# A macaron layer with a state-space scan on one core: tanh for silu, and products with tokens on partitions

## The chip, the core and the metric

The kernel runs on one core of a Trainium2 chip. Its engines are TensorE (PE), VectorE (DVE), ScalarE (ACT), GpSimd (POOL) and SyncE (SP), which issues transfers. The metric is the device time of one launch in microseconds (us), smaller is better. The time before is 2232.82 us, the median of 3 runs (2228.62 to 2250.01).

## The reference, cut to what matters

32 sequences of 256 tokens with 128 channels go through three layers, each behind a layer norm and added to its input: half an FFN, a Mamba block, half an FFN (the same weights both times). All of it is float32.

```
ffn(x):    router = x @ Wg ; top_logits, idx = top_k(router, 2)          # of 8 experts
           w = scatter(softmax(top_logits))                              # (tokens, 8)
           h = silu(x W1[e]) * (x W2[e])          # 8 experts of 176 hidden columns
           y = sum_e w[:, e] * (h W3[e]) + (silu(x Ws1) * (x Ws2)) Ws3   # shared: 352 columns
mamba(x):  x_in, z = split(x W_in + b_in)                                # 256 channels each
           xc = silu(causal_conv4(x_in) + conv_b)
           B, C = split(xc W_xp + b_xp) ; delta = softplus(xc W_dt + b_dt)
           h_t = exp(delta_t A) h_{t-1} + delta_t xc_t B_t               # 16 states
           y = (sum_states(h_t C_t) + D_skip xc) * silu(z)
           return layernorm(x + y W_out + b_out, alpha, beta)
x = x + 0.5 ffn(norm(x)) ; x = x + mamba(norm(x)) ; x = x + 0.5 ffn(norm(x))
```

## The kernel before, in words

**Tiling.** Two sequences, 512 tokens, are one group; there are 16 groups, and nearly all products have their 512 tokens as columns. Pass k works on five groups at once: FFN 1 of group k+2 (the diff says it `enters`), the projections of the Mamba block of k+1 (`lead`), the scan of k (`scans`), the output projection of k-1 (`tail`) and FFN 2 of k-2 (`last`). Passes -2 to 1 and 14 to 17 are written out and only partly filled; passes 2 to 13 are full and run in a hardware loop of two passes an iteration.

**A pass has 32 slots.** Each engine runs its own program of the same slots, and semaphores tie them together. In each pair of slots one of the 16 scan states is worked on: at the start of the even slot PE lays the row of B out over the partitions (`row_b`, L1012, into `ps_db`); DVE multiplies it with `du` at the end of the slot before (`input_term`, L834, which waits for the row), runs the scan (L868) in the even slot, and GpSimd multiplies with the row of C (`prod`, L569). ScalarE makes the decays, two Exp a state (L657).

**FFN units.** The hidden columns of an FFN are 14 chunks: 3 of shared columns, then 11 of experts. One chunk is a unit and starts in each of slots 0 to 13 (FFN 2) or 14 to 27 (FFN 1). In its slot PE makes `ps_h1` (L1030) and `ps_h2` (L1048), each a 512-column product into one of two banks, and ScalarE makes `silu` from `ps_h1` (L680). One slot later DVE makes `gated`: `ps_h2` times the routing weights `wrow` for an expert chunk, times silu for a shared one (L860). Two slots later GpSimd multiplies an expert chunk with silu (the join, L521). Four slots later PE adds the down product (L1043) to `ps_y`, channels on partitions. `ps_h1` is free for the next but one unit when silu has read it, `ps_h2` when DVE has.

**Other steps** are put in slots by a table written by hand, `PLAN` (and `SP_PLAN` for transfers). In a slot each engine first does the scan's and the unit's work, then the steps of the table in their order. Nearly all of PE's other products (`xT`, `logits`, `wT`, `in0` to `in3`, `dt`, `xproj`, `cT`, `bT`, `outproj`, `outT`, `yT`) go to one PSUM bank, `ps_m`: PE claims it for a step only when the step before in the table has been read out (`claim` waits for `misc_taken`), and the reader waits for `misc_full`. The steps that the change touches:
- `y0`/`y1` (ACT, L730): copies `ps_y` to `yT`; `yT0`/`yT1` (PE): four transposes; `addy` (DVE, L926): adds half of it to `xres`.
- `in0`, `in1` (x_in with the convolution as four shifted products, L1003, and an edge product) and `in2`, `in3` (z): ScalarE makes silu of them straight from `ps_m`.
- `outproj` (PE, L1110, two products of 512 columns with channels on partitions; ACT copies to `oT` and adds `b_out`), `outT` (four transposes), `resid` (DVE, L961, adds it to `rtok`), `stats3` (DVE).
- `x1n` (ACT): makes the normalised input of the Mamba block once more, into `rtok`.
- `dt0`, `dt1`: softplus on ScalarE: Abs (L752) and Identity (L750) of each half, Exp (L756), and in the next slot Ln (L668).
- `route` and `weights`: the two largest logits, and the softmax of them. GpSimd makes the power of e (L542), DVE the sum (L912), the quotient and two products.

Exp, Ln and silu need tables in ScalarE; where the next function is in another set than the one loaded, an ACT_TABLE_LOAD stands ahead of it in the program.

## Time and profile before

| | |
|---|---|
| median of 3 runs (range) | 2232.82 us (2228.62 to 2250.01) |
| profiled execution: time, span | 2241.29 us, 2239.5 us |
| mean granted TensorE clock | 0.887 |
| busy share PE / DVE / ACT / POOL | 80% / 73% / 69% / 64% |
| chain that ended last | PE 43%, ACT 21%, DVE 17%, issue 12% |
| instructions | 22836 |

Read the shares with care: an engine with 70% may be full in one stretch of a pass and idle in the next, so the page's first part names the candidates, and the windows over one pass show which engine is full where. In the timeline, the time in square brackets is how long the engine stood idle before the row, and behind it what it waited for.

### The profile page before, as it was taken

The page shows a single profiled execution, that of the slowest core. Times are in us where ns is not written, and L with a number is a line of the kernel's source. Part 1 is how long each engine was busy: PE and PEld are TensorE (multiplying, and loading weights), DVE is VectorE, ACT ScalarE, POOL GpSimd, SP SyncE. Part 2 cuts the span into 40 slices and gives each one's busy share as a digit, 9 for nine tenths or more (in the row PEclk, how much of TensorE's full clock was granted, in tenths as well). Part 3 has the DMA queues.
Part 4 walks back from the last instruction along what each step waited for, and adds up shares of the span by engine and source line. Part 5 has one row for each costly group of instructions (what it writes and reads, how often), then busy time and mean ns, then how long its engine had stood idle before and what let it go on. Part 6 is the DMA issues. An engine that isn't in the chain of part 4 may idle for free.

```text
span 2239.5 us, 22836 instructions
## 1 busy us (share of the span) xinstructions
PE 1794.9 (80%) x4674; PEld 804.4 (36%) x4674; DVE 1639.6 (73%) x2505; ACT 1535.3 (69%) x2083; POOL 1441.3 (64%) x1286
## 2 busy tenths in 40 slices
PE   3878587979888888887888798788888878885577
PEld 1433233434334333333433343333333433332233
DVE  2257878687786878878687877878778786879742
ACT  1257587777778767786876778687677867776522
POOL 3346676666667675776767666676766676676753
PEclk9989788989898898998989898898989889897698
DMA  4117565555556555555555654655556555557642
GB/s 130 45 55 178 119 164 130 144 133 143 127 142 153 130 135 134 152 132 151 152 137 129 152 143 127 151 147 140 130 131 159 131 145 138 133 122 173 150 111 61
DMA packets 119129, 300.05 MB, mean 134 GB/s; under 512 B 19184, under 2 KB 40400, under 8 KB 104656
## 3 DMA queue, kind: packets, MB, share of 16 engines
q0 software_dynamic: 18432, 125.84, 28.1%
q1 hardware_dynamic: 92672, 168.88, 24.2%
q10 hardware_dynamic: 7888, 4.09, 0.7%
q14 instruction: 123, 1.01, 0.1%
q8 instruction: 14, 0.23, 0.0%
HBM read 167.67 MB, written 5.24 MB: 77 GB/s over the span
## 4 chain that ended last, share of the span: by engine, by line
PE 43%; ACT 21%; DVE 17%; issue 12%; POOL 3%; ACTq 1%; DMA 1%; DVEq 0%; POOLq 0%
PE ps_y L1043 9%; PE ps_h2a L1048 6%; DVE hist L868 5%; PE ps_m L1003 5%; ACT L680 5%; PE ps_h1a L1030 4%; PE ps_h1b L1030 4%; ACT L657 4%; PE ps_h2b L1048 4%; DVE den L912 3%; ACT decay L657 3%; ACT silu L680 2%; DVE yacc L950 2%; PE ps_m L1110 2%; DVE ps_db L834 2%
## 5 line engine op out<-in xcount | busy, mean ns | idle before, releaser
L569 POOL TENSOR_TENSOR prod<-hist,crow 128x1024 f32<-128x1024 f32 x224 | 556.0, 2482 | 371.8 <-DVE hist L868 368.0
L1043 PE MATMUL ps_y<-gated,down_w 128*128 128x512 f32 (+1 forms) x896 | 517.6, 664 | 101.3 <-POOL gated L521 63.2
L868 DVE TENSOR_TENSOR_SCAN hist<-decay,ps_db 128x1024 f32<-128x1024 f32 x256 | 583.2, 2278 | 13.8 <-issue 11.3
L521 POOL TENSOR_TENSOR gated<-gated,silu 128x512 f32<-128x512 f32 x352 | 476.3, 1416 | 138.1 <-DVE gated L860 108.4
L834 DVE TENSOR_TENSOR ps_db<-du,ps_db 128x1024 f32<-128x1024 f32 x256 | 313.7, 1225 | 319.1 <-PE ps_db L1012 318.8
L657 ACT ACTIVATE decay<-delta,a_neg 128x510 f32<-128x510 f32 x512 | 338.1, 711 | 2.6
L1048 PE MATMUL ps_h2a<-xnT,up_w 128*128 128x512 f32 (+1 forms) x448 | 253.2, 649 | 53.3 <-DVE gated L860 53.3
L680 ACT ACT_TABLE_LOAD x227 | 291.2, 1283 | 5.5 <-issue 0.7
L1043 PEld LDWEIGHTS ps_y<-gated,down_w 128*128 128x128 f32 (+1 forms) x896 | 180.3, 209 | 319.3 <-issue 218.0
L1030 PE MATMUL ps_h1a<-xnT,up_w 128*128 128x512 f32 (+1 forms) x448 | 248.0, 636 | 49.7 <-ACT silu L680 48.8
L657 ACT ACT_TABLE_LOAD x217 | 278.4, 1283 | 3.8
L1030 PE MATMUL ps_h1b<-xnT,up_w 128*128 128x512 f32 x448 | 240.1, 618 | 38.8 <-ACT silu L680 38.5
L1048 PE MATMUL ps_h2b<-xnT,up_w 128*128 128x512 f32 x448 | 235.9, 609 | 0.0
L680 ACT ACTIVATE silu<-ps_h1a 128x512 f32<-128x512 f32 (+1 forms) x224 | 132.8, 593 | 57.6 <-PE ps_h1a L1030 57.3
L680 ACT ACTIVATE silu<-ps_h1b 128x512 f32<-128x512 f32 x224 | 133.8, 597 | 48.3 <-PE ps_h1b L1030 43.1
L1012 PE MATMUL ps_db<-bT,sel_b 96*128 96x512 bf16 x256 | 108.3, 423 | 69.4 <-DVE hist L868 69.3
L860 DVE TENSOR_TENSOR gated<-ps_h2b,wrow 128x512 f32<-128x512 f32 x192 | 131.2, 683 | 41.2 <-PE ps_h2b L1048 41.2
L860 DVE TENSOR_TENSOR gated<-ps_h2a,wrow 128x512 f32<-128x512 f32 x160 | 108.5, 678 | 68.2 <-PE ps_h2a L1048 64.8
L1048 PEld LDWEIGHTS ps_h2a<-xnT,up_w 128*128 128x128 f32 (+1 forms) x448 | 89.0, 202 | 183.0 <-issue 109.8
L718 ACT ACTIVATE bounce<-ps_m 8x512 f32<-8x512 f32 x32 | 18.8, 587 | 184.7 <-PE ps_m L993 184.7
L1030 PEld LDWEIGHTS ps_h1b<-xnT,up_w 128*128 128x128 f32 x448 | 81.4, 196 | 134.7 <-issue 69.2
L1003 PE MATMUL ps_m<-xnT,w_conv 128*128 128x512 f32 (+3 forms) x256 | 121.9, 621 | 6.6 <-DVE rtok L961 4.2
(137 smaller groups left out, 2242.5 us busy)
## 6 DMA issues: line engine op xcount, KB each, us to landing
yacc<-prod POOLq DMA_DIRECT2D x112, 1024.0 KB, 9.0
crow<-c_rows SPq DMA_DIRECT2D x128, 512.0 KB, 4.2
wrow<-w_rows SPq DMA_DIRECT2D x320, 128.0 KB, 3.6
wrow<-w_rows SPq DMA_DIRECT2D x64, 224.0 KB, 3.2
wrow<-w_rows SPq DMA_DIRECT2D x64, 192.0 KB, 3.6
wrow<-w_rows SPq DMA_DIRECT2D x64, 160.0 KB, 3.4
yacc<-yacc POOLq DMA_DIRECT2D x16, 512.0 KB, 6.2
wrow<-w_rows SPq DMA_DIRECT2D x64, 96.0 KB, 3.3
```

Of the source, the lines that this page charges most:

```text
L521: nc.gpsimd.tensor_tensor(gated[:, pos % NGATE, :], gated[:, pos % NGATE, :], silu[:, (pos + NCHUNK * f_parity(k, f)) % NSILU, :], ALU.mul ...
L569: nc.gpsimd.tensor_tensor(prod[:, (pair - 1 + odd) % 2, s % 2, :, :], hist[:, s % 2, :, :], c_all, ALU.mult).then_inc(prod_done, 1)
L657: ins = nc.scalar.activation(decay[:, s % NA, half, :, 1:LEN], d[:, :, 1:LEN], ACT.Exp, scale=a_neg[:, half, s:s + 1])
L680: nc.scalar.activation(silu[0:r, (pos + NCHUNK * f_parity(k, f)) % NSILU, :], ps_h1[pos % 2][0:r, :], ACT.Silu).then_inc(silu_done, 1)
L834: nc.vector.tensor_tensor(ps_db[:].rearrange("p (h t) -> p h t", h=HALVES), du[par][:], ps_db[:, TG:2 * TG].unsqueeze(1).to_broadcast([P, ...
L860: nc.vector.tensor_tensor(gated[0:r, pos % NGATE, :], ps_h2[pos % 2][0:r, :], factor, ALU.mult).then_inc(h2_taken, 1)
L868: nc.vector.tensor_tensor_scan(hist[:, s % 2, :, :].rearrange("p h t -> p (h t)"), decay[:, s % NA, :, :, :].rearrange("p h b t -> p (h b ...
L1003: nc.tensor.matmul(acc[:, :, late:LEN], w_conv[:, tap, half * P:(half + 1) * P], now[:, :, 0:LEN - late], start=(tap == PAD), stop=False)
L1012: nc.tensor.matmul(ps_db[:, TG:2 * TG], sel_b[:, s, :], bT[par][:], start=True, stop=True).then_inc(b_full, 1)
L1030: nc.tensor.matmul(ps_h1[pos % 2][0:r, :], up_w[:, 0, j * P:j * P + r], xnT[f][:], start=True, stop=True).then_inc(h1_full, 1)
L1043: nc.tensor.matmul(ps_y[:], down_w[0:rd, jd, :], gated[0:rd, posd % NGATE, :], start=(posd == 0), stop=(posd == NCHUNK - 1)).then_inc(down ...
L1048: nc.tensor.matmul(ps_h2[pos % 2][0:r, :], up_w[:, 1, j * P:j * P + r], xnT[f][:], start=True, stop=True).then_inc(h2_full, 1)
```

## The change

What it does, in five parts:
- ScalarE makes Tanh of half of `h1` instead of silu. DVE makes (tanh + 1) times `ps_h1` in place (`scalar_tensor_tensor`), twice the silu; so `addy` multiplies with 0.25 in place of 0.5. The same for `in0` to `in3`: Tanh and Identity on ScalarE, then a new step `gate0` to `gate3` on DVE, which frees `ps_m`. Tanh is in the set of Exp.
- The down product and the output projection have tokens on partitions: four (eight) products of 128 columns, whose stationary side is the 128x128 block of `gated` (`yacc`). `y`, `yT` and `outT` go, `addy` reads `ps_y` directly, and `b_out` becomes a product with one row.
- The sums, quotients and products of `weights` move from DVE to GpSimd.
- `x1n` is no longer made again: SP copies the kept one by a transfer (`keep_x1n`).
- The steps stand in other slots (`PLAN`, `SP_PLAN`).

```diff
     PLAN = {
-        0: ["stats0", "y0"], 1: ["yT0", "x1n"], 2: ["addy0", "norm0"], 3: ["stats2", "fold"], 4: ["xT0"],
-        5: ["logits0", "norm2"], 6: ["route0", "gate_y"], 7: ["xT2"], 8: ["weights0", "outproj"], 9: ["in0"],
-        10: ["wT0"], 11: ["outT"], 12: ["resid"], 13: ["in1", "stats3"], 14: ["in2"],
-        15: ["in3", "ln_norm"], 17: ["y1"], 18: ["dt0", "stats1"], 19: ["dt1"], 20: ["yT1", "norm1"],
-        21: ["addy1"], 22: ["xproj", "delta"], 23: ["bparts"], 24: ["xT1"], 25: ["logits1"], 26: ["route1"],
-        27: ["cT"], 28: ["bT", "weights1"], 30: ["wT1"],
+        0: ["stats0", "addy0"], 1: ["stats2"], 2: ["norm0"], 3: ["norm2", "fold"], 4: ["xT0"], 5: ["logits0"],
+        6: ["route0", "xT2"], 7: ["gate_y"], 8: ["weights0"], 9: ["outproj"], 10: ["resid", "in0", "stats3"],
+        11: ["gate0"], 12: ["wT0", "in1"], 13: ["gate1"], 14: ["in2", "ln_norm"], 15: ["gate2"], 16: ["in3"],
+        17: ["gate3", "addy1", "stats1"], 18: ["dt0"], 19: ["dt1", "norm1"], 21: ["xproj"],
+        22: ["delta", "bparts", "xT1"], 23: ["logits1"], 24: ["route1"], 25: ["cT"], 26: ["weights1", "bT"],
+        29: ["wT1"],
     }
...
+                            sp.dma_start(rtok[:], x1n[odd][:]).then_inc(x1n_ready, 16)
...
+                        elif step == "weights0" and enters(k) or step == "weights1" and tail(k):
+                            chain.link(nc.gpsimd.tensor_tensor(den[:], edrop[:], pow_mone[:], ALU.subtract))
+                            chain.link(nc.gpsimd.tensor_tensor(prob[:, :, 0], den[:], pow_mone[:], ALU.pow))
+                            chain.link(nc.gpsimd.tensor_tensor(prob[:, :, 1], edrop[:], prob[:, :, 0], ALU.mult))
...
-                        elif step in ("in0", "in1") and lead(k):
+                        elif step in ("in0", "in1", "in2", "in3") and lead(k):
...
+                            nc.scalar.activation(gate, ps_m[:], ACT.Tanh, bias=b_half[:, c:c + 1], scale=0.5
+                                                 ).then_inc(gate_tanh, 1)
+                            act.wait_ge(gate_tanh, n)
+                            nc.scalar.activation(gate, gate, ACT.Identity, bias=pow_half[:, 0:1], scale=0.5
+                                                 ).then_inc(gate_ready, 1)
...
                         nc.vector.tensor_tensor(gated[0:r, pos % NGATE, :], ps_h2[pos % 2][0:r, :], factor, ALU.mult
                                                 ).then_inc(h2_taken, 1)
+                        if j < ECHUNK:
+                            dve.wait_ge(tanh_done, n + 1)
+                            nc.vector.scalar_tensor_tensor(act_half, act_half, 1.0, ps_h1[pos % 2][0:r, :],
+                                                           ALU.add, ALU.mult).then_inc(silu_done, 1)
...
-                            nc.vector.scalar_tensor_tensor(xr, ps_m[:], 0.5, xr, ALU.mult, ALU.add
+                            nc.vector.scalar_tensor_tensor(xr, ps_y[:], 0.25, xr, ALU.mult, ALU.add
+                                                           ).then_inc(y_taken, 1)
+                        elif step in ("gate0", "gate1", "gate2", "gate3") and lead(k):
+                            nc.vector.scalar_tensor_tensor(gate, ps_m[:], bias, gate, ALU.add, ALU.mult
                                                            ).then_inc(misc_taken, 1)
...
-                        nc.tensor.matmul(ps_y[:], down_w[0:rd, jd, :], gated[0:rd, posd % NGATE, :], start=(posd == 0),
-                                         stop=(posd == NCHUNK - 1)).then_inc(down_done, 1)
+                        for t in range(TILES):
+                            ins = nc.tensor.matmul(ps_y[:, t * C:(t + 1) * C],
+                                                   gated[0:rd, posd % NGATE, t * P:(t + 1) * P], down_w[0:rd, jd, :],
+                                                   start=(posd == 0 and t == 0),
+                                                   stop=(posd == NCHUNK - 1 and t == TILES - 1))
+                        ins.then_inc(down_done, 1)
...
+                            nc.tensor.matmul(ps_m[:].rearrange("p (t c) -> p t c", t=TILES), ones_r[:],
+                                             b_out_r[:].unsqueeze(1).to_broadcast([1, TILES, C]), start=True,
+                                             stop=False)
+                            for t in range(TILES):
+                                for half in range(HALVES):
+                                    ins = nc.tensor.matmul(ps_m[:, t * C:(t + 1) * C],
+                                                           yacc[nxt][:, 0, half, t * P:(t + 1) * P],
+                                                           w_out[:, half, :], start=False,
+                                                           stop=(t == TILES - 1 and half == HALVES - 1))
```

**PE, slots 8 to 10.** The rows below are PE's order in the loop before, from the output projection in slot 8 (L1110) to the next input row (`ps_db`, L1012); the semaphore that a row waits for stands behind it.

```order
L1110 MATMUL ps_m<-yacc,w_out 128x512 [waits misc_taken]
L1110 MATMUL ps_m<-yacc,w_out 128x512
...
L1030 MATMUL ps_h1b<-xnT,up_w 128x512 [waits silu_done]
...
L1043 MATMUL ps_y<-gated,down_w 128x512 [waits weighted]
L1048 MATMUL ps_h2b<-xnT,up_w 128x512 [waits h2_taken]
...
L1003 MATMUL ps_m<-xnT,w_conv 128x512 [waits misc_taken]
L1003 MATMUL ps_m<-xnT,w_conv 128x2x255
L1003 MATMUL ps_m<-xnT,w_conv 128x2x254
L1003 MATMUL ps_m<-xnT,w_conv 128x2x253
L1005 MATMUL ps_m<-edge,edge_w 128x2x3
```

The changed kernel, from `ps_h2` of slot 9 to the convolution of `in0`, which now stands in slot 10:

```order
L1065 MATMUL ps_h2b<-xnT,up_w 128x512 [waits h2_taken]
...
L1121 MATMUL ps_m<-b_out_r,ones_r 128x512 [waits misc_taken]
L1126 MATMUL ps_m<-w_out,yacc 128x128 x8
...
L1025 MATMUL ps_db<-bT,sel_b 128x512 [waits scan_done]
...
L1043 MATMUL ps_h1a<-xnT,up_w 128x512 [waits silu_done]
...
L1057 MATMUL ps_y<-down_w,gated 128x128 [waits weighted]
L1057 MATMUL ps_y<-down_w,gated 128x128 x3
L1065 MATMUL ps_h2a<-xnT,up_w 128x512 [waits h2_taken]
...
L1016 MATMUL ps_m<-xnT,w_conv 128x512 [waits misc_taken]
...
L1018 MATMUL ps_m<-edge,edge_w 128x2x3
```

Before, the convolution claimed `ps_m` from ScalarE's copy `oT`; now it claims it from DVE's `resid`, one slot after the output projection, and behind it stand the products of the next unit.

**DVE, slots 10 to 13.** Before, from the input term that ends slot 11 (L834) to the statistics of `rtok`:

```order
L834 TENSOR_TENSOR ps_db<-du,ps_db 128x1024 [waits scan_done,b_full]
...
L860 TENSOR_TENSOR gated<-ps_h2b,wrow 128x512 [waits w_ready0]
L868 SCALAR_TENSOR_TENSOR hist<-decay,ps_db 128x1024 [waits prod_done,decay_ready,dbx_done]
...
L961 TENSOR_TENSOR rtok<-rtok,ps_m 128x512 [waits misc_full]
...
L860 TENSOR_TENSOR gated<-ps_h2a,wrow 128x512 [waits w_ready1,down_done,h2_full]
L796 MEMSET carrier_s 128x1 [waits misc_taken,pads_zero]
L798 BN_STATS bnst<-rtok 128x6 x4
```

The changed kernel, from the gate product of slot 10 (L875) with its silu operation (L879) to the input term that ends slot 11 (L845):

```order
L875 TENSOR_TENSOR gated<-ps_h2b,wrow 128x512 [waits w_ready2,down_done,h2_full]
...
L887 SCALAR_TENSOR_TENSOR hist<-decay,ps_db 128x1024 [waits prod_done,decay_ready,dbx_done]
...
L974 TENSOR_TENSOR rtok<-rtok,ps_m 128x512 [waits misc_full]
L809 MEMSET carrier_s 128x1 [waits misc_taken,pads_zero]
L811 BN_STATS bnst<-rtok 128x6 x4
...
L814 MEMSET carrier 128x1 [waits dve_stats]
L816 BN_AGGR mvr<-bnst 128x2 x4
...
L875 TENSOR_TENSOR gated<-ps_h2a,wrow 128x512 [waits w_ready3,down_done,h2_full]
L879 SCALAR_TENSOR_TENSOR silu<-silu,ps_h1a 128x512 [waits tanh_done]
...
L939 SCALAR_TENSOR_TENSOR xconv<-ps_m,b_conv,xconv 128x512 [waits gate_ready]
...
L845 TENSOR_TENSOR ps_db<-du,ps_db 128x1024 [waits scan_done,b_full]
```

`resid` (`rtok<-rtok,ps_m`) stood in slot 12 and stands in slot 10 now, behind the scan; `gate0` (`xconv<-ps_m`) is new, and each unit has a silu operation behind its gate product.

**ACT, slots 19 and 20.** Before, from `dt1` (L750) to the decays of slot 20 (L657):

```order
L750 ACTIVATE dtmp<-ps_m,b_dt_c 128x512 [waits misc_full]
L752 ACTIVATE dpre<-ps_m,b_dt_c 128x512
...
L756 ACT_TABLE_LOAD
L756 ACTIVATE dtmp<-dtmp 128x1024 [waits softplus_chain]
L668 ACT_TABLE_LOAD
L668 ACTIVATE dtmp<-dtmp 128x1024 [waits softplus_chain]
...
L680 ACT_TABLE_LOAD [waits h2_taken]
L680 ACTIVATE silu<-ps_h1a 128x512 [waits h1_full]
L644 ACTIVATE xn<-xres,nbias,rstd 128x128 [waits nbias_ready1,pads_zero]
L644 ACTIVATE xn<-xres,nbias,rstd 128x128 x3
...
L657 ACT_TABLE_LOAD
L657 ACTIVATE decay<-delta,a_neg 128x2x255 [waits scan_done]
```

The changed kernel, from `dt1` (L760) to the decays (L679) of slot 20:

```order
L760 ACTIVATE dtmp<-ps_m,b_dt_c 128x512 [waits misc_full]
L762 ACTIVATE dpre<-ps_m,b_dt_c 128x512
...
L766 ACTIVATE dtmp<-dtmp 128x1024 [waits softplus_chain]
...
L666 ACTIVATE xn<-xres,nbias,rstd 128x128
...
L690 ACT_TABLE_LOAD
L690 ACTIVATE dtmp<-dtmp 128x1024 [waits softplus_chain]
...
L702 ACT_TABLE_LOAD [waits h2_taken]
L702 ACTIVATE silu<-ps_h1a 128x512 [waits h1_full]
...
L679 ACTIVATE decay<-delta,a_neg 128x2x255 [waits scan_done]
L679 ACTIVATE decay<-delta,a_neg 128x2x255
```

Ahead of silu and of the decays no load is left but the one that follows Ln, and `norm1` (four rows `xn<-xres`, one shown) stands ahead of Ln now. The whole program has 151 rows of ACT_TABLE_LOAD before and 13 after (a row in the loop body counts once).

## Rows read from the trace of the kernel before

**Rows 1.** The page, part 1 (busy us, share, instructions) and part 4
```profile
PE 1794.9 (80%) x4674; PEld 804.4 (36%) x4674; DVE 1639.6 (73%) x2505; ACT 1535.3 (69%) x2083; POOL 1441.3 (64%) x1286
...
PE 43%; ACT 21%; DVE 17%; issue 12%; POOL 3%; ACTq 1%; DMA 1%; DVEq 0%; POOLq 0%
```

**Rows 2.** The page, part 5: table loads ahead of silu
```profile
L680 ACT ACT_TABLE_LOAD x227 | 291.2, 1283 | 5.5 <-issue 0.7
```

**Rows 3.** Windows (stretch, length, busy us (count) by engine, clock): A to F; loop
```profile
1279.12:1310.88 31.76, 24.36 (x68) 10.84 (x67) 26.88 (x56) 29.57 (x44) 22.79 (x24) 0.95 0.59 154
1310.88:1337.66 26.78, 26.65 (x68) 12.11 (x69) 19.57 (x29) 16.85 (x21) 17.48 (x15) 0.94 0.64 152
1337.66:1350.12 12.46, 12.46 (x31) 5.40 (x30) 9.29 (x8) 9.91 (x15) 9.00 (x11) 1.00 0.61 163
1350.12:1371.15 21.03, 17.82 (x38) 7.22 (x36) 11.08 (x20) 14.71 (x19) 14.05 (x13) 0.84 0.52 128
1371.15:1384.69 13.54, 10.39 (x30) 5.73 (x31) 11.94 (x13) 13.39 (x18) 10.18 (x8) 0.75 0.62 169
1384.69:1412.18 27.49, 20.98 (x60) 8.99 (x58) 24.38 (x34) 15.13 (x21) 15.94 (x13) 0.81 0.38 90
...
357.20:1941.20 1584.00, 1333.20 (x3505) 597.60 (x3505) 1241.03 (x1872) 1194.28 (x1597) 1074.92 (x949) 0.90 0.55 140
```

**Rows 4.** Timeline of PE (start, length, operation, [idle before <-releaser]), prices
```profile
1324.59 0.60 PE L993 MATMUL ps_m<-ident,wtok 128*8 128x128 f32 x4
...
1325.02 1.02 PE L1030 MATMUL ps_h1b<-xnT,up_w 128*128 128x512 f32 x2
1325.88 1.02 PE L1043 MATMUL ps_y<-gated,down_w 128*128 128x512 f32 x2
...
1333.42 3.58 PE L1003 MATMUL ps_m<-xnT,w_conv 128*128 128x512 f32 x8
...
1387.06 0.60 PE L993 MATMUL ps_m<-ident,xn 128*128 128x128 f32 x4
1387.50 1.02 PE L1030 MATMUL ps_h1b<-xnT,up_w 128*128 128x512 f32 x2
```

**Rows 5.** Timeline of DVE, slots 10 to 13
```profile
1328.45 1.23 DVE L834 TENSOR_TENSOR ps_db<-du,ps_db 128x1024 f32<-128x1024 f32 x1 [1.65 <-PE ps_db L1012]
1329.59 0.68 DVE L860 TENSOR_TENSOR gated<-ps_h2b,wrow 128x512 f32<-128x512 f32 x1
1330.19 2.28 DVE L868 TENSOR_TENSOR_SCAN hist<-decay,ps_db 128x1024 f32<-128x1024 f32 x1
1332.39 0.66 DVE L961 TENSOR_TENSOR rtok<-rtok,ps_m 128x512 f32<-128x512 f32 x1
1332.97 0.68 DVE L860 TENSOR_TENSOR gated<-ps_h2a,wrow 128x512 f32<-128x512 f32 x1
...
1337.66 1.23 DVE L834 TENSOR_TENSOR ps_db<-du,ps_db 128x1024 f32<-128x1024 f32 x1 [2.80 <-PE ps_db L1012]
```

**Rows 6.** Groups by line and form (count, busy, mean ns, idle); DVE timeline
```profile
L926 DVE SCALAR_TENSOR_TENSOR xres<-ps_m,xres 128x512 f32 x24 | 16.1, 672 | 0.0
...
L950 DVE SCALAR_TENSOR_TENSOR yacc<-xconv,d_c,yacc 128x512 f32<-128x512 f32 x32 | 54.2, 1735 | 6.7 <-DMA yacc<-yacc 6.3
...
1401.77 5.50 DVE L912 TENSOR_SCALAR den<-edrop 128x4 f32<-128x4 f32 x1
```

**Rows 7.** Timeline of PE where it stands in stretches D and F
```profile
1354.11 2.05 PE L1043 MATMUL ps_y<-gated,down_w 128*128 128x512 f32 x2 [3.17 <-ACT yT L730]
...
1402.56 2.07 PE L1043 MATMUL ps_y<-gated,down_w 128*128 128x512 f32 x2 [3.73 <-POOL gated L521]
```

**Rows 8.** Timeline of ACT round the softplus of slot 20
```profile
1368.92 1.06 ACT L756 ACTIVATE dtmp<-dtmp 128x1024 f32<-128x1024 f32 x1
...
1374.14 1.64 ACT L644 ACTIVATE xn<-xres,nbias,rstd 128x128 f32 x4
```

**Rows 9.** Groups by line and form: GpSimd's power
```profile
L542 POOL TENSOR_TENSOR edrop<-euler,drop 128x4 f32<-128x4 f32 x32 | 32.9, 1029 | 2.5
```

145 lines of the change are left out of this document (65 added, 80 removed), and 6 rows, old and new, of the table SP_PLAN.

## The prediction

> **What bounds the kernel now.** I read the page first. No engine is full: TensorE (PE) 80%, VectorE (DVE) 73%, ScalarE (ACT) 69%, GpSimd (POOL) 64%, and the chain of waits goes over PE 43%, ACT 21%, DVE 17% [rows 1]. ScalarE's share is the one the change attacks: 227 table loads of 1283 ns, 291 us, in front of silu alone [rows 2], and about as many in front of exp when it switches back, of 1535 us in all. Read alone that is a quarter of the span. What it is worth is read from the stages.
>
> The loop body runs 12 times between 357.2 and 1941.2 us, 132.0 us a pass [rows 3]; the 655 us outside are partly filled passes. I cut one pass into six stretches, each starting with an input term (L834) of an even slot [rows 3]: A slots 0–7 (31.8 us), B 8–13 (26.8), C 14–17 (12.5), D 18–21 (21.0), E 22–23 (13.5), F 24–31 (27.5), together 133.1. Their busy times show who binds. In B and C PE works without a gap (26.65 of 26.78, 12.46 of 12.46), so ScalarE's loads cost nothing there. In A and E DVE and ACT are both near full. In D and F nobody is: PE stands 3.17 us for ACT's copy yT (D) and 3.73 us for GpSimd's product (F) [rows 7], and DVE stands 5.50 us in a 128x4 operation [rows 6]. The change can win in A, D and F, and can only lose in B and C.
>
> **Prices.** TensorE: one 512-column fp32 product is two passes, 0.86 us start to start (1325.02 to 1325.88) [rows 4]. The new down product is four products of 128 columns, eight passes, each with its own stationary load; before has none of these. Nearest are the transposes: four with 128 stationary columns take 0.44 us (1387.06 to 1387.50), four with 8 columns 0.43 us (1324.59 to 1325.02) [rows 4]. So a 128-column load hides behind a 128-column pass, and the new product costs 8 x 0.11 = 0.86 to 0.88: nothing changes. If each load were added to its pass, it would be 1.7. The three removed transposes (yT0, yT1, outT) give 1.3 us a pass, the bias product takes 0.86.
>
> The Trainium skill ("TensorE: Matmul & The Clock Gate", Part 3) says that a weight load overlaps running matmuls only when its row group differs. By that the 0.44 and 0.43 should stand far apart; they don't, but transposes are not two-pass products, so the rule stays as a rival with a small chance.
>
> VectorE: the new silu operation has one operand in PSUM, one in SBUF. L926 has the same kinds: 672 ns [rows 6], and as with the gate products the next one starts 0.60 us on (1329.59 to 1330.19) [rows 5]. The upper bound is 1.74 us, L950 with both operands in SBUF [rows 6]; I take 0.60. Per pass 28 such and four for the gates: +19.2 us, on DVE's 103.1 (its six entries in [rows 3]). Removed are the routing sums, of which the stall of 5.50 us is the largest. So DVE goes to some 113 to 117 us a pass.
>
> ScalarE loses some 28 loads a pass (227 over 16 groups, and again as many); the instruction order keeps two, round Ln. GpSimd gets five small operations per routing; the power is 1.03 us [rows 9], the others far smaller, with the links between them I take 2.5 us, twice a pass.
>
> **The sum, stretch by stretch.**
> A: DVE 26.9 and seven silu operations, 4.2, give 31.1; the silu waits go, PE's logits behind slot 5 still cost about 1. 32.4 (31.1 to 33.5).
>
> B: here the moved steps bite. All `ps_m` steps share one bank, each claims it only when the step before has been taken. Before, out product, copy and transpose stood at slots 8 and 11, in0 at 9, in1 at 13, with two units between resid and in1. Now outproj is at 9, and in0 stands in slot 10, behind resid, which DVE does in slot 10 after the scan. From the start of slot 8's input term: the bank of h1 comes free after input term 1.14, gate 0.60, silu 0.67: 2.4. PE's three products of slot 9 (3 x 0.86) and outproj (bias and eight 128-column products, 2.57): 7.5. Row product and start of DVE 0.43. Then input term 1.14, gate and silu 1.2, scan 2.20 [rows 5], resid 0.67: 13.2, while PE was through slot 10's products at 10.3. **PE waits 2.9 us.** The convolution of in0, 3.58 for its eight passes [rows 4] and about 3.8 with the edge product: 17.0. Slot 11: 19.6. Slot 12: products 2.8, wT0's transposes 0.43, about 1.0 until ScalarE has copied them, in1 3.8: 27.6. Slot 13 and 0.43: 30.7. PE idles 3.9 and 2.9 us in it. After 3.73 us idle the pair at 1402.56 [rows 7] took 2.07 us where one of a busy stretch took 1.02 (1325.88) [rows 4], at half clock; I add 2: 32.7 (26.8, if the waits do not open, to 36).
>
> C: DVE 9.3, four silu, two gates, and addy1 and stats1, moved here from D: 0.60, and 1.3, which is what stats3 takes between the gate product at 1332.97 and the wait of 2.80 us ahead of 1337.66 [rows 5]. 14.7. PE needs 12.5. 14.7 (14.5 to 15.5).
>
> D: the wait for yT is gone. Slots 18–19 have ten 512-column products and a row product, 8.8 of PE work, 1.6 of it beside DVE's tail of C: 7.2. At 20 the softplus still stands ahead of tanh: from Exp, by way of Ln, two loads and silu, to norm1 it is 5.2 us now (1368.92 to 1374.14) [rows 8]. Abs and Identity stand ahead (512 elements each: by the 1.06 for Exp's 1024 some 1.2 together), and norm1, 1.64, now stands between Exp and Ln. So tanh of slot 20 ends 8.1 us behind dt1, and its silu operation comes behind that: 8.8. Together 16.0 (15 to 18).
>
> E: DVE 11.9 and 1.2: 13.1. xT1 moved to slot 22, where its bank waits for bparts, behind delta. PE idles about 7 us, then comes back at half clock with logits1 still to do: 15.0 (13.1 to 15.7).
>
> F: the 5.50 us stall goes, five silu operations come (3.0). But GpSimd ends last here (the 3.73), and gets 2.5 us of sums ahead of its last products: of 5.5 I keep 1.4. 26.1 (22 to 28).
>
> Sum 136.9 for 133.1: +3.8 a pass, +46 us in 12 passes. The partly filled passes I leave alone (±10). The profiled execution took 2241.3 us; 2241 + 46 = 2287, and the median lies 8.5 us below it: **2280 us**. One per cent is about what a measurement of this kernel can tell from no change.
>
> **The rivals.**
> 1. Forecast, slower: DVE's 19 us and B's one-bank waits cost more than ScalarE gives back. For it: B and C are full of PE work today. Against it: D and F lose 6.4 us that are seen as waits. 2255 to 2345. Chance 0.46.
> 2. Faster: B's waits do not open. It decides whether resid is done when PE is through slot 10; if so, B stays at 26.8 and the sum is 131.0: -25 us, 2207. If GpSimd is also in time in F (23) and E stays DVE's (13.5), 126.4: -80, 2153. For it: the input terms of before still wait for PE, 1.65 and 2.80 us in [rows 5], room that silu operations can fill for nothing. Chance 0.30, middle 2180.
> 3. Half of the waits open: within 1%, 2211 to 2255. Chance 0.19.
> 4. Weight loads are not hidden: 0.86 more for each of 28 products, 24 us of PE a pass; on the path in B and D and half of C and A, about 10: +120 us, 2400. Against it the two transpose rows. Chance 0.05.
> That the loads stay is ruled out by the order, which has them round Ln alone.
>
> **The numbers.** 2280 is case 1's. 2155 to 2345 takes in cases 1 to 3 and leaves out case 4 and the far end of 2; the likeliest case's own range is 2255 to 2345. Faster 0.30, same 0.19, slower 0.51.
>
> **What would show it.** Table loads near 40; down products at 0.86 to 0.88 us a unit (1.7: case 4). In B: PE idle ahead of in0's convolution (L1016), released by DVE rtok, about 2.9 us, and B near 32; no such idle: case 2. D near 16, with DVE waiting for ACT's tanh at slot 20. F near 26 with PE released by POOL; 23 says that I overrated GpSimd. DVE near 115 us a pass; 130 would mean silu operations stretched towards L950. If ScalarE holds more than a tenth of the chain, I misread which waits its loads leave.

## The result and the profile after

| | before | predicted | after |
|---|---|---|---|
| time, median (us) | 2234.21 (4 runs) | 2280 (2155 to 2345) | 2523.2 (2516.8 to 2523.91, 4 runs) |
| ratio to before | | 1.02 | 1.1274 [1.1214, 1.1334] |
| span of the profiled execution | 2239.5 | | 2521.9 |
| one pass of the loop, mean of 12 | 132.00 | 136.9 | 150.86 |
| outside the 12 passes | 655 | 655 | 712 |

Slower was forecast, but the loss is 289 us and not 46. The page of the changed kernel, as in [rows 1]:

```profile
span 2521.9 us, 28261 instructions
...
PE 1871.0 (74%) x7394; PEld 1099.8 (44%) x7394; DVE 1836.8 (73%) x2859; ACT 933.9 (37%) x1587; POOL 1509.3 (60%) x1447
...
PE 40%; DVE 23%; issue 16%; POOL 12%; ACT 5%; DMA 2%; ACTq 1%; DVEq 1%; POOLq 0%
```

ScalarE is now 37% busy for 69% and holds 5% of the chain for 21%. Its table loads are as good as gone: by the groups of lines there are 33 where there were 481, of which 31 stand round Ln. So the change does what it says, and still loses. The windows over the six stretches of one pass of the loop, cut and read as in [rows 3] (A to F; the numbers are length, busy us and count of PE, PE's weight loads, DVE, ACT and POOL, and the granted clock):

```profile
1289.07:1325.95 36.88, 26.75 (x96) 14.03 (x96) 33.26 (x62) 15.39 (x29) 25.05 (x26) 0.91 0.59 151
1325.95:1361.53 35.58, 29.61 (x106) 16.47 (x107) 20.67 (x32) 8.48 (x14) 20.24 (x22) 0.86 0.42 105
1361.53:1381.54 20.01, 14.71 (x56) 8.63 (x55) 14.94 (x26) 9.08 (x17) 10.80 (x8) 0.91 0.39 102
1381.54:1398.45 16.91, 15.74 (x73) 9.56 (x72) 11.55 (x14) 12.17 (x19) 11.21 (x11) 1.00 0.63 160
1398.45:1413.70 15.25, 8.87 (x38) 6.02 (x39) 13.30 (x15) 4.05 (x7) 8.80 (x6) 0.78 0.67 170
1413.70:1439.99 26.29, 19.74 (x97) 13.82 (x95) 21.18 (x34) 8.91 (x15) 17.83 (x18) 0.87 0.35 88
```

Over all 12 passes (worked out from the starts of the input terms in DVE's timeline), with the runs that the next part tells of:

| us a pass | A 0–7 | B 8–13 | C 14–17 | D 18–21 | E 22–23 | F 24–31 | sum |
|---|---|---|---|---|---|---|---|
| before | 31.9 | 26.7 | 12.5 | 20.3 | 13.5 | 27.2 | 132.0 |
| predicted | 32.4 | 32.7 | 14.7 | 16.0 | 15.0 | 26.1 | 136.9 |
| after | 35.8 | 35.1 | 20.1 | 17.8 | 15.8 | 26.3 | 150.9 |
| run 1: ln_norm 15 | 35.9 | 35.3 | 15.5 | 15.7 | 16.2 | 26.2 | 144.9 |
| run 2: outproj 8 | 35.9 | 28.7 | 20.1 | 18.1 | 15.9 | 26.3 | 144.9 |
| run 3: both moves | 35.9 | 28.7 | 15.5 | 15.7 | 15.9 | 26.3 | 138.1 |
| run 6: before, Tanh alone | 28.7 | 27.4 | 12.5 | 14.6 | 12.9 | 25.5 | 121.5 |
| run 7: before, Tanh and DVE | 34.2 | 29.7 | 13.2 | 16.0 | 13.8 | 28.1 | 134.9 |
| run 9: before, tokens | 33.0 | 27.0 | 12.8 | 14.6 | 13.6 | 26.7 | 127.7 |
| run 10: before, tokens and gates | 33.0 | 30.1 | 16.7 | 14.6 | 13.5 | 27.2 | 135.2 |
| run 14: best | 30.9 | 26.8 | 12.8 | 14.6 | 13.7 | 26.1 | 124.9 |

E and F came out within 1 us of the forecast; A, B, C and D did not. **C** is read on three engines. GpSimd in slots 13 to 16:

```profile
1357.63 2.49 POOL L528 TENSOR_TENSOR gated<-gated,silu 128x512 f32<-128x512 f32 x2
1368.06 1.28 POOL L572 TENSOR_TENSOR rtok<-rtok,alpha_b 128x512 f32<-128x512 f32 x1 [7.94 <-ACT rtok L666]
...
1372.15 2.35 POOL L591 TENSOR_TENSOR prod<-hist,crow 128x1024 f32<-128x1024 f32 x1
...
1375.79 1.58 POOL L528 TENSOR_TENSOR gated<-gated,silu 128x512 f32<-128x512 f32 x1
```

GpSimd stands 7.94 us for ScalarE's part of `ln_norm` (L666, the normalised `rtok`), does its own three operations, then the product of state 7, a transfer, and only then the join of unit 13, the last of FFN 2 (1375.79). The last down product of FFN 2 waits for that join, and PE works in order (first row: `h1` of slot 17; second: the down product):

```profile
1371.10 1.02 PE L1043 MATMUL ps_h1b<-xnT,up_w 128*128 128x512 f32 x2
1377.42 2.07 PE L1057 MATMUL ps_y<-down_w,gated 128*128 128x128 f32 x8 [5.30 <-POOL gated L528]
```

and behind PE stands DVE, whose `addy1` reads `ps_y` in slot 17, with the input term of slot 18 behind it:

```profile
1374.68 0.74 DVE L939 SCALAR_TENSOR_TENSOR zs<-ps_m,b_in_c,zs 128x512 f32<-128x512 f32 x1
1379.72 0.69 DVE L931 SCALAR_TENSOR_TENSOR xres<-ps_y,xres 128x512 f32 x1 [4.30 <-PE ps_y L1057]
```

**The border of A and B** on PE, slots 9 and 10, and on DVE, slots 7 to 11:

```profile
1328.41 2.08 PE L1043 MATMUL ps_h1b<-xnT,up_w 128*128 128x512 f32 x2 [5.68 <-DVE silu L879]
1330.27 1.91 PE L1057 MATMUL ps_y<-down_w,gated 128*128 128x128 f32 x8
...
1333.27 1.12 PE L1121 MATMUL ps_m<-b_out_r,ones_r 1*128 1x512 f32 x2
1334.32 2.05 PE L1126 MATMUL ps_m<-w_out,yacc 128*128 128x128 f32 x16
...
1341.87 5.38 PE L1016 MATMUL ps_m<-xnT,w_conv 128*128 128x512 f32 x8 [2.67 <-DVE rtok L974]
```

```profile
1319.37 2.63 DVE L963 SCALAR_TENSOR_TENSOR yacc<-xconv,d_c,yacc 128x512 f32<-128x512 f32 x2
1322.03 3.99 DVE L967 TENSOR_TENSOR yacc<-yacc,zs 128x1024 f32<-128x1024 f32 x1
1325.95 1.22 DVE L845 TENSOR_TENSOR ps_db<-du,ps_db 128x1024 f32<-128x1024 f32 x1
1327.08 0.68 DVE L875 TENSOR_TENSOR gated<-ps_h2b,wrow 128x512 f32<-128x512 f32 x1
1327.68 0.67 DVE L879 SCALAR_TENSOR_TENSOR silu<-silu,ps_h1b 128x512 f32<-128x512 f32 x1
...
1349.08 0.75 DVE L939 SCALAR_TENSOR_TENSOR xconv<-ps_m,b_conv,xconv 128x512 f32<-128x512 f32 x1 [4.66 <-ACT xconv L754]
```

DVE does `gate_y` (6.6 us, 1319.37 to 1325.95), the input term and a gate product before the silu operation that frees the bank of `h1` for slot 9 (1327.68). PE waits 5.68 us for it and comes back at half clock: 2.08 and 1.91 us where a busy stretch has 1.02 and 1.05. Only behind these stands the output projection of slot 9; `resid` follows it, so PE waits another 2.67 us and the convolution takes 5.38 us. The granted clock (the first number behind GpSimd's count) of the two stretches behind these waits:

```profile
1328.41:1332.00 3.59, 3.59 (x11) 2.56 (x12) 3.31 (x3) 0.60 (x1) 1.28 (x1) 0.50 0.55 145
1341.87:1347.20 5.33, 5.33 (x9) 2.05 (x9) 2.42 (x12) 0.00 (x0) 3.56 (x7) 0.68 0.00 0
```

A granted clock of 0.50 is 1.2 of 2.4 GHz: the first stretch runs at the lower level throughout, the second, at 0.68, partly. Then DVE waits 4.66 us for the two ScalarE operations ahead of `gate0`.

The new down product is no cause; from its start to that of `h2` it is 0.89 us:

```profile
1362.19 1.05 PE L1057 MATMUL ps_y<-down_w,gated 128*128 128x128 f32 x8
1363.08 1.02 PE L1065 MATMUL ps_h2a<-xnT,up_w 128*128 128x512 f32 x2
```

### The profile page after: what moved, and what is told of

It is laid out like the page before. It is cut to its first block, busy times and chain, and to the rows that moved or that the text cites. A ratio compares the mean times of both kernels' runs of the same rounds, so it can differ in the third digit from the quotient of the medians.

```text
span 2521.9 us, 28261 instructions
## 1 busy us (share of the span) xinstructions
PE 1871.0 (74%) x7394; PEld 1099.8 (44%) x7394; DVE 1836.8 (73%) x2859; ACT 933.9 (37%) x1587; POOL 1509.3 (60%) x1447
## 4 chain that ended last, share of the span: by engine, by line
PE 40%; DVE 23%; issue 16%; POOL 12%; ACT 5%; DMA 2%; ACTq 1%; DVEq 1%; POOLq 0%
PE ps_y L1057 9%; DVE hist L887 9%; PE ps_m L1016 6%; PE ps_h1b L1043 5%; PE ps_h2b L1065 5%; POOL prod L591 4%; POOL gated L528 3%; PE ps_h1a L1043 3%; DVE ps_db L845 3%; PE ps_h2a L1065 3%; DVE silu L879 2%; PE ps_m L1105 2%; PE ps_m L1006 2%; DMA yacc<-prod 2%; DVE yacc L963 2%
## 5 line engine op out<-in xcount | busy, mean ns | idle before, releaser
L1057 PEld LDWEIGHTS ps_y<-down_w,gated 128*128 128x128 f32 (+1 forms) x3584 | 533.0, 216 | 374.3 <-issue 194.5
L1057 PE MATMUL ps_y<-down_w,gated 128*128 128x128 f32 (+1 forms) x3584 | 540.9, 301 | 148.9 <-POOL gated L528 148.5
L887 DVE TENSOR_TENSOR_SCAN hist<-decay,ps_db 128x1024 f32<-128x1024 f32 x256 | 583.4, 2279 | 14.7 <-issue 12.2
L845 DVE TENSOR_TENSOR ps_db<-du,ps_db 128x1024 f32<-128x1024 f32 x256 | 313.4, 1224 | 263.5 <-PE ps_db L1025 263.2
L1043 PE MATMUL ps_h1b<-xnT,up_w 128*128 128x512 f32 x448 | 273.5, 696 | 88.8 <-DVE silu L879 78.5
L679 ACT ACTIVATE decay<-delta,a_neg 128x510 f32<-128x510 f32 x512 | 335.2, 708 | 5.1 <-DVE hist L887 5.1
L1043 PE MATMUL ps_h1a<-xnT,up_w 128*128 128x512 f32 (+1 forms) x448 | 262.5, 670 | 90.9 <-DVE silu L879 52.6
L1065 PE MATMUL ps_h2b<-xnT,up_w 128*128 128x512 f32 x448 | 247.9, 637 | 0.0
L1016 PE MATMUL ps_m<-xnT,w_conv 128*128 128x512 f32 (+3 forms) x256 | 144.5, 718 | 51.6 <-DVE rtok L974 38.9
L1043 PEld LDWEIGHTS ps_h1a<-xnT,up_w 128*128 128x128 f32 (+1 forms) x448 | 83.1, 200 | 161.3 <-DVE silu L879 69.8
L875 DVE TENSOR_TENSOR gated<-ps_h2b,wrow 128x512 f32<-128x512 f32 x192 | 131.1, 683 | 26.3 <-PE ps_h2b L1065 26.3
L879 DVE SCALAR_TENSOR_TENSOR silu<-silu,ps_h1a 128x512 f32<-128x512 f32 x160 | 108.1, 676 | 38.6 <-ACT silu L702 38.6
L879 DVE SCALAR_TENSOR_TENSOR silu<-silu,ps_h1b 128x512 f32<-128x512 f32 x192 | 129.8, 676 | 0.0
L875 DVE TENSOR_TENSOR gated<-ps_h2a,wrow 128x512 f32<-128x512 f32 x160 | 107.6, 672 | 27.4 <-PE ps_h2a L1065 26.2
L939 DVE SCALAR_TENSOR_TENSOR xconv<-ps_m,b_conv,xconv 128x512 f32<-128x512 f32 x32 | 24.0, 751 | 136.2 <-ACT xconv L754 136.2
```

Of the source, the lines that this page charges most:

```text
L679: ins = nc.scalar.activation(decay[:, s % NA, half, :, 1:LEN], d[:, :, 1:LEN], ACT.Exp, scale=a_neg[:, half, s:s + 1])
L845: nc.vector.tensor_tensor(ps_db[:].rearrange("p (h t) -> p h t", h=HALVES), du[par][:], ps_db[:, TG:2 * TG].unsqueeze(1).to_broadcast([P, ...
L875: nc.vector.tensor_tensor(gated[0:r, pos % NGATE, :], ps_h2[pos % 2][0:r, :], factor, ALU.mult).then_inc(h2_taken, 1)
L879: nc.vector.scalar_tensor_tensor(act_half, act_half, 1.0, ps_h1[pos % 2][0:r, :], ALU.add, ALU.mult).then_inc(silu_done, 1)
L887: nc.vector.tensor_tensor_scan(hist[:, s % 2, :, :].rearrange("p h t -> p (h t)"), decay[:, s % NA, :, :, :].rearrange("p h b t -> p (h b ...
L1016: nc.tensor.matmul(acc[:, :, late:LEN], w_conv[:, tap, half * P:(half + 1) * P], now[:, :, 0:LEN - late], start=(tap == PAD), stop=False)
```

## The experiments

The kernel before was timed beside every run; its median was 2231 to 2236 us. What a run gives back or costs is the difference of medians, and the ratio is to the kernel before.

**1. `ln_norm` back in slot 15.**

```diff
-        11: ["gate0"], 12: ["wT0", "in1"], 13: ["gate1"], 14: ["in2", "ln_norm"], 15: ["gate2"], 16: ["in3"],
+        11: ["gate0"], 12: ["wT0", "in1"], 13: ["gate1"], 14: ["in2"], 15: ["gate2", "ln_norm"], 16: ["in3"],
```

> The changed kernel with one entry of the table moved: ln_norm stands in slot 15 again (behind GpSimd's join of the last expert chunk of FFN 2), not in slot 14. Theory 'late join': in the changed kernel GpSimd stands 7.9 us for ScalarE's ln_norm in slot 14, the join of unit 13 comes behind it, PE stands 5.3 us ahead of the last down product, and DVE's addy1 with the input term behind it stands 4.3 us. Then slots 14 to 17 fall from 20.1 to 15 or 16 us and the time to 2445 to 2470 us. Rival 'PE': C is long because PE's work in it is slow (weight loads, clock); then slots 14 to 17 keep 20 us and the time stays at 2515 to 2525.

2444.6 us, ratio 1.0941 [1.0907, 1.0976]: 79 us back by one word of the table. On GpSimd the join now stands ahead of the three operations:

```profile
1329.83 1.59 POOL L528 TENSOR_TENSOR gated<-gated,silu 128x512 f32<-128x512 f32 x1
1331.07 1.58 POOL L572 TENSOR_TENSOR rtok<-rtok,alpha_b 128x512 f32<-128x512 f32 x1
```

and PE at the last down product of FFN 2 there:

```profile
1331.05 1.02 PE L1043 MATMUL ps_h1b<-xnT,up_w 128*128 128x512 f32 x2
1331.91 1.05 PE L1057 MATMUL ps_y<-down_w,gated 128*128 128x128 f32 x8
```

The down product follows `h1` without a gap. C falls from 20.1 to 15.5 and D, which had the delay handed on, from 17.8 to 15.7. "Late join" is shown; "PE" falls.

**2. The output projection one slot earlier.**

```diff
-        6: ["route0", "xT2"], 7: ["gate_y"], 8: ["weights0"], 9: ["outproj"], 10: ["resid", "in0", "stats3"],
+        6: ["route0", "xT2"], 7: ["gate_y"], 8: ["weights0", "outproj"], 9: ["resid"], 10: ["in0", "stats3"],
```

> The changed kernel with outproj in slot 8, resid in slot 9 and in0 and stats3 in slot 10 (the change has 9, 10, 10, 10). Theory 'one bank, read by DVE': PE is idle 5.7 us in slot 8 and could do the output projection there, resid is then read before PE comes to in0, so the 2.7 us wait ahead of the convolution and the half clock in it (5.38 for 3.58 us) go; slots 8 to 13 fall from 35.1 to 28 to 31 us, the time to 2440 to 2480. Rival 'silu on DVE': PE stands in 8 to 13 for the silu operations of DVE whatever stands in ps_m; then under 1 us a pass, 2505 to 2525.

2438.3 us, 1.0908 [1.0874, 1.0941]: 85 us back. PE in slots 8 to 10:

```profile
1286.06 2.06 PE L1121 MATMUL ps_m<-b_out_r,ones_r 1*128 1x512 f32 x2 [3.43 <-DVE yacc L967]
1288.06 3.78 PE L1126 MATMUL ps_m<-w_out,yacc 128*128 128x128 f32 x16
...
1297.35 3.58 PE L1016 MATMUL ps_m<-xnT,w_conv 128*128 128x512 f32 x8
```

PE still idles for `gate_y`, but the projection now fills the rest of that time. It runs at half clock (0.50 granted); by the convolution the granted clock is 1.00 again, and the convolution starts without a wait and takes 3.58 us. B falls from 35.1 to 28.7, as expected. The rival falls.

**3. Both moves.** 

> The changed kernel with both moves of the two runs before: ln_norm in slot 15; outproj in 8, resid in 9, in0 in 10. If the two losses lie apart (slots 14 to 17, slots 8 to 13), the gains of 79 and 85 us add up: 2350 to 2370 us, 138 to 139 us a pass. Rival: what waits no longer in one place waits in the other (DVE or GpSimd is the bound behind both): 2390 to 2430 us. In either case still slower than the kernel before, so that the rest is to be sought in slots 0 to 7 and 18 to 23.

2349.4 us, 1.0515 [1.0472, 1.0559]. The gains add up, and 10 us more (79 + 85 = 164; 174 measured). What is left over the kernel before is 115 us. In the profiled executions it is 108: 73 in the loop, where A, B, C and E are 2.0 to 4.0 us a pass longer and D 4.6 us shorter, and 35 outside it.

**4. `gate_y` in slot 6 on top of both.**

```diff
-        6: ["route0", "xT2"], 7: ["gate_y"], 8: ["weights0", "outproj"], 9: ["resid"], 10: ["in0", "stats3"],
+        6: ["route0", "gate_y"], 7: ["xT2"], 8: ["weights0", "outproj"], 9: ["resid"], 10: ["in0", "stats3"],
```

> The changed kernel with both moves and gate_y back in slot 6, behind route0 (xT2 in slot 7). In the changed kernel its product with zs took 3.6 us in slot 7, beside GpSimd's work, and 1.23 us in slot 6 of the kernel before. If it is the neighbour on GpSimd that stretches it, it goes back to 1.2 to 1.5 us and the pass loses 2 to 3 us: 2315 to 2335 us. Rival: DVE is full there anyway and the operation only meets another of GpSimd's: 2350 to 2370 us.

2359.7 us, 1.0558 [1.0514, 1.0602]: no gain, 10 us worse. The operation did shrink (second row):

```profile
1237.54 3.49 DVE L963 SCALAR_TENSOR_TENSOR yacc<-xconv,d_c,yacc 128x512 f32<-128x512 f32 x2
1241.07 1.23 DVE L967 TENSOR_TENSOR yacc<-yacc,zs 128x1024 f32<-128x1024 f32 x1
```

but PE's wait behind `gate_y` now stands at `h1` of slot 8, ahead of the projection, which can no longer fill it:

```profile
1243.54 2.07 PE L1043 MATMUL ps_h1a<-xnT,up_w 128*128 128x512 f32 x2 [6.24 <-DVE silu L879]
```

A gives 2.0 us a pass, B takes 2.4, and the loop is as long as in run 3. So the stretched operation is real, but shortening it alone gains nothing here: PE's wait behind `gate_y` moves along with it.

**5. The changed kernel without DVE's silu operation.**

```diff
-                                             ps_h1[pos % 2][0:r, :], ACT.Tanh, scale=0.5).then_inc(tanh_done, 1)
+                                             ps_h1[pos % 2][0:r, :], ACT.Tanh, scale=0.5).then_inc(silu_done, 1)
...
-                        if j < ECHUNK:
-                            dve.wait_ge(tanh_done, n + 1)
-                            nc.vector.scalar_tensor_tensor(act_half, act_half, 1.0, ps_h1[pos % 2][0:r, :],
-                                                           ALU.add, ALU.mult).then_inc(silu_done, 1)
```

> The changed kernel without the (tanh + 1) times h1 operation of the 28 FFN units a pass (left out: the product with h1; tanh itself is used as silu); ScalarE's tanh frees the bank of h1, as silu did before. It takes 28 x 0.60 = 17 us a pass off DVE and gives PE back the slack of before. Theory 'DVE is the price': 12 to 17 us a pass come back, most in slots 0 to 7, where the 5.7 us wait of PE behind gate_y goes: 2300 to 2370 us. Rival 'placement': the loss is in the moved steps (ln_norm, outproj, resid), and slots 8 to 17 keep their length: 2410 to 2470 us.

2409.8 us, 1.0782 [1.0749, 1.0815]: 113 us, 7.8 us a pass where "DVE is the price" wanted 12 or more. A and B give 2.6 and 2.7 us, C nothing. The time ends at the edge of "placement", though B did not keep its length as that had it. GpSimd's late join and the late projection are still there, so part of DVE's time given back is probably waited away; no run shows how much.

**6 and 7. The exchange by itself, in the old table.** First the loads alone: `ACT.Silu` becomes `ACT.Tanh` in the kernel before, in all places, and the factor that makes silu of it is left out. Then also the multiplication on DVE for the 28 FFN units a pass, as in the changed kernel.

> The kernel before with Tanh in place of Silu wherever it stands (left out: the factor that makes silu of it), so that nearly all table loads go and nothing else changes. It says what the loads alone were worth. By the stretches, ScalarE ends last only in parts of slots 0 to 7, 18 to 21 and 22 to 23: 4 to 7 us a pass, 2140 to 2185 us. Rival: the loads stand beside other work everywhere: 2215 to 2235 us. Rival: they were a tenth of the time or more: under 2020 us.

> The kernel before with the exchange of engines alone: Tanh on ScalarE and the (tanh + 1) times h1 operation on DVE for the 28 FFN units a pass, in the old slots and with the old products (left out: in0 to in3 take Tanh for silu). Against the 2109 us of the run with Tanh alone it gives the price of the DVE operations in the old table. Theory 'half hidden': as in the changed kernel, where taking them out gave 7.8 us a pass, 110 to 130 us come on top: 2215 to 2245 us, so that the exchange by itself gains nothing. Rival 'placement': in the old slots DVE has room in 8 to 21 and in 24 to 31, and only 0 to 7 pay: 2140 to 2180 us.

2109.4 us, 0.9435 [0.9406, 0.9465], and 2298.9 us, 1.0281 [1.0237, 1.0324]. So the loads were worth 125 us, more than I expected, and all of it in A, D, E and F: B and C don't get shorter, as their full PE said. The DVE operations then cost 190 us, also more than either expectation. In the loop DVE's busy time grows by 203 us (1226.22 to 1429.28), and the loop by 161, four fifths of the added work. What PE waited for `h1` and `h2` in one pass (us in total, times, longest), with Tanh alone:

```profile
PE ps_h2a L1048 <- DVE gated L860: 4.2, 2, 3.7
...
PE ps_h2b L1048 <- DVE gated L860: 2.1, 1, 2.1
...
PE ps_h1a L1030 <- ACT silu L680: 0.5, 1, 0.5
```

and with the DVE operation, in the longest pass of that run (138.8 us):

```profile
PE ps_h1a L1040 <- DVE silu L870: 10.4, 3, 6.4
...
PE ps_h1a L1040 <- DVE silu L854: 4.0, 1, 4.0
...
PE ps_h1b L1040 <- DVE silu L870: 1.7, 2, 1.0
```

Without it `h1` is freed by ScalarE and PE waits 0.5 us for it; with it, 16.1 us, the longest 6.4 us behind `gate_y`. But the waits for `h2`, 6.3 us, are gone: PE now stands at `h1`, which DVE frees too. Over all 12 passes, PE's waits for both banks grow from 6.7 to 14.1 us a pass, those for GpSimd's join from 2.7 to 5.6, and PE's own work takes 4.1 us longer at a granted clock of 0.91 for 0.93; that is the loop's 13.4 us a pass but for 1 us that other waits get shorter. The exchange loses 65 us by itself.

**8. Is it the bank or DVE's time?** The run before, with PE's down product ahead of `h1` in each slot.

```diff
                     u = up_unit(k, slot)
-                    if u is not None:
...
-                        nc.tensor.matmul(ps_h1[pos % 2][0:r, :], up_w[:, 0, j * P:j * P + r], xnT[f][:],
-                                         start=True, stop=True).then_inc(h1_full, 1)
                     d = back_unit(k, slot)
...
+                    if u is not None:
...
+                        nc.tensor.matmul(ps_h1[pos % 2][0:r, :], up_w[:, 0, j * P:j * P + r], xnT[f][:],
+                                         start=True, stop=True).then_inc(h1_full, 1)
```

> The kernel before with the exchange alone (Tanh on ScalarE, multiplication on DVE for the FFN units; in0 to in3 take Tanh for silu), and PE's down product ahead of the h1 product in each slot. Theory 'bank of h1': the 13 us a pass that the DVE operations cost are PE's wait for ps_h1, which is now freed behind the gate product in DVE's order; 0.86 us of other work ahead of each wait hides a part: 3 to 8 us a pass, 2190 to 2260 us. Rival 'DVE is full': it is DVE's own time, and PE's order doesn't matter: 2285 to 2310 us. Rival: the down product, which waits for GpSimd's join, now holds h1: over 2310 us.

2289.1 us, 1.0262 [1.0198, 1.0325]: 10 us of the 190, in the range of "DVE is full". Over the 12 passes PE's waits for `h1` do fall, from 169 to 142 us, but its waits for GpSimd's join rise from 67 to 92: the third rival holds in part. DVE holds 35% of the chain, for 34% in run 7 and 17% in [rows 1]. So most of PE's wait moves along when its order changes. That agrees with DVE's own time as the price, but one change of order does not prove it.

**9. The down product on tokens alone, with silu on ScalarE.** In the kernel before: the four products of the change; `y`, `yT` go; `addy` reads `ps_y`.

```diff
-        0: ["stats0", "y0"], 1: ["yT0", "x1n"], 2: ["addy0", "norm0"], 3: ["stats2", "fold"], 4: ["xT0"],
+        0: ["stats0"], 1: ["x1n"], 2: ["addy0", "norm0"], 3: ["stats2", "fold"], 4: ["xT0"],
...
-        15: ["in3", "ln_norm"], 17: ["y1"], 18: ["dt0", "stats1"], 19: ["dt1"], 20: ["yT1", "norm1"],
-        21: ["addy1"], 22: ["xproj", "delta"], 23: ["bparts"], 24: ["xT1"], 25: ["logits1"], 26: ["route1"],
+        15: ["in3", "ln_norm"], 17: ["addy1"], 18: ["dt0", "stats1"], 19: ["dt1"], 20: ["norm1"],
+        22: ["xproj", "delta"], 23: ["bparts"], 24: ["xT1"], 25: ["logits1"], 26: ["route1"],
```

> The kernel before with the down product on tokens alone (four products of 128 columns; the copy yT and its transposes go, addy reads ps_y, addy1 in slot 17, addy0 in slot 2; silu, output projection and all other slots as before). Theory: a unit takes 0.89 us on PE as in the changed kernel, the 3.2 us wait for yT goes: 2 to 4 us a pass, 2175 to 2210 us. Rival 'weight loads': slots 8 to 17, full of PE work, get longer by 0.1 to 0.9 us a unit: 2240 to 2350 us. Rival 'addy1 on DVE': addy1 in slot 17 waits for the last down product and holds the input term behind it: slots 16 to 17 grow from 5.4 to 8 or more, and the gain is used up: 2225 to 2250 us.

2187.9 us, 0.9796 [0.9747, 0.9845]: a gain of 46 us. It is D (20.3 to 14.6); A takes 1.1 us a pass back. Both rivals fall: C, full of PE work, grows by 0.3 us only, and slots 16 to 17 from 5.4 to 5.6.

**10. The gates alone, on top of 9.** `in0` to `in3` as in the changed kernel (Tanh, Identity, then DVE).

```diff
-        10: ["wT0"], 11: ["outT"], 12: ["resid"], 13: ["in1", "stats3"], 14: ["in2"],
-        15: ["in3", "ln_norm"], 17: ["addy1"], 18: ["dt0", "stats1"], 19: ["dt1"], 20: ["norm1"],
+        10: ["gate0", "wT0"], 11: ["outT"], 12: ["resid"], 13: ["in1", "stats3"], 14: ["gate1", "in2"],
+        15: ["gate2", "in3", "ln_norm"], 16: ["gate3"], 17: ["addy1"], 18: ["dt0", "stats1"], 19: ["dt1"], 20: ["norm1"],
```

> The kernel before with the down product on tokens and the new way of in0 to in3 alone: Tanh and Identity on ScalarE, the product on DVE one slot later (gate0 to gate3 in slots 10, 14, 15, 16), which frees ps_m; silu of the FFN units as before. Theory 'bank freed by DVE': ps_m is held by the chain ScalarE, ScalarE, DVE in place of one ScalarE operation, in slots in which PE was full, so PE waits for it: 3 to 5 us a pass, 2230 to 2260 us, half or more of the 80 us that the changed kernel with silu back on ScalarE and both moves is over the one with tokens alone. Rival 'fewer loads': in0 to in3 need no table of their own now, and DVE has room in slots 8 to 17: 2165 to 2195 us.

2300.4 us, 1.03 [1.0244, 1.0356]: 112 us more than 9, for four DVE operations a pass of 0.7 us. PE, slots 10 and 14:

```profile
1364.63 1.02 PE L1067 MATMUL ps_h2a<-xnT,up_w 128*128 128x512 f32 x2
1367.79 0.60 PE L1008 MATMUL ps_m<-ident,wtok 128*8 128x128 f32 x4 [2.14 <-DVE xconv L941]
...
1382.52 1.02 PE L1067 MATMUL ps_h2a<-xnT,up_w 128*128 128x512 f32 x2
1385.68 1.13 PE L1105 MATMUL ps_m<-xnT,w_in 128*128 128x512 f32 x2 [2.14 <-DVE xconv L941]
```

and DVE in slot 10:

```profile
1364.82 2.28 DVE L875 TENSOR_TENSOR_SCAN hist<-decay,ps_db 128x1024 f32<-128x1024 f32 x1
1367.01 0.73 DVE L941 SCALAR_TENSOR_TENSOR xconv<-ps_m,b_conv,xconv 128x512 f32<-128x512 f32 x1
```

`ps_m` was taken by a ScalarE operation right behind the product; now it is taken by DVE, behind a gate product and a scan. PE, which had no gap in B and C, waits 2.14 us in each of two places; slots 10 to 11 and 14 to 15 grow by 3.0 us each. It is more than the theory's 3 to 5 us a pass: 7.5. Over the 12 passes, 90 us longer, these two waits are 51 us; the other 39 are PE's work taking longer, at a granted clock of 0.91 for 0.93. In nine of the passes PE does some products behind one of the two waits at half clock, and slots 10 to 11 or 14 to 15 are 1.7 us longer by it. The rest of the 112 lies outside the loop. Nothing comes back on ScalarE: 475 table loads are left of 481, since only five stood at `in0` to `in3`.

**11 to 13. The other parts, and the decays.** Run 11 is 3 with silu back on ScalarE for the FFN units. Runs 12 and 13 are 9 with the decays made for two states at a time, then also with the routing sums on GpSimd:

```diff
-    DECAYS = {2 * s - 4: s for s in range(2, NS)}
+    DECAYS = {4 * i - 2: [2 * i, 2 * i + 1] for i in range(1, NS // 2)}
```

> The changed kernel with both moves (ln_norm 15; outproj 8, resid 9), and with silu of the 28 FFN units back on ScalarE (table loads and all), without their DVE operation; in0 to in3 keep Tanh and the DVE gates. If the exchange costs here what it cost in the old table (2299 against 2234), it gives 50 to 80 us back: 2270 to 2300 us. Rival: with the loads back, the waits of ScalarE come on top of the gates and the new slots: 2330 to 2400 us.

> The kernel before with the down product on tokens (as in the run before) and the decays made for two states at a time, once in four slots in place of once in two: ScalarE then switches tables half as often, 14 fewer loads a pass of silu's and Exp's together or more, and DVE gets nothing on top. Theory: what the loads cost in slots 0 to 7 (33.0 us, against 28.7 without loads) comes back by half or more: 2 to 5 us a pass, 2115 to 2160 us, faster than both kernels. Rival: four decays in a row hold silu, and with it the bank of h1, by 5 us in every fourth slot: 2180 to 2220 us.

> As the run with tokens and pairs, with the routing sums on GpSimd in place of DVE, as in the changed kernel. It takes the 128x4 operation off DVE that stood 5.5 us, and gives GpSimd about 3 us twice a pass. Theory 'GpSimd ends slots 24 to 31': the joins there are late by the sums, and what DVE gains is given back: within 10 us of the run without it. Rival 'the stall was on the path': slots 24 to 31 fall by 2 to 4 us, 25 to 50 us faster.

Run 11: 2267.7 us, 1.0175 [1.0111, 1.0239]. Taking the exchange out gives 82 us back here too, near the 65 of the old table. What is left over run 9 (80 us) lies in the other parts, which no run divides in the new table: the gates less the routing sums, the output projection, the transfer for `x1n`, and the slots. Run 12: 2212.3 us, 0.991 [0.9885, 0.9936]: 24 us worse than 9, the rival was right in B, C and E (1.0 to 1.2 us each), and only A got shorter (33.0 to 31.2). Run 13: 2195.9 us, 0.9838 [0.9776, 0.99]: the sums on GpSimd are a gain of 16 us, between what theory (10 at most) and rival (25 to 50) said, and 1.1 us of its 1.8 a pass lie in A; in F slots 28 to 29 fall from 10.3 to 7.0 and 30 to 31 rise from 4.1 to 6.8.

**14. The parts that pay, together.** Run 9, the routing sums on GpSimd, pairs of decays in slots 2 and 6 alone.

```diff
+    DECAYS = {2 * s - 4: [s] for s in range(6, NS)} | {2: [2, 3], 6: [4, 5]}
```

> The kernel before with the down product on tokens, the routing sums on GpSimd, and the decays of two states at a time in slots 2 and 6 alone (states 2 to 5), where ScalarE's loads were on the path; silu stays on ScalarE. Pairs everywhere gave slots 0 to 7 back 1.8 us and lost 3.4 us in slots 8 to 23; the routing sums gave 16 us. If both hold apart: 2188 - 23 - 16, 2140 to 2160 us, faster than every kernel so far. Rival: GpSimd's sums only paid beside the pairs of slots 24 to 31: 2170 to 2195 us.

2151.9 us, 0.9636 [0.9584, 0.9688]: as expected, and the fastest of all kernels here that compute the whole layer: 79 us under the kernel before, timed beside it, and 371 under the changed one. Its page:

```profile
PE 1746.3 (81%) x7234; PEld 1045.1 (49%) x7234; DVE 1506.3 (70%) x2345; ACT 1445.5 (67%) x1995; POOL 1502.1 (70%) x1446
...
PE 44%; issue 14%; DVE 13%; POOL 13%; ACT 12%; DMA 2%; ACTq 1%; DVEq 0%; POOLq 0%; SPq 0%
```

PE's share of the chain is back at 44%, with ScalarE still making silu, loads and all.

## Why the prediction was wrong

**What was right.** That it is slower, for the two reasons given (runs 2, 7 and 10 show the one bank and DVE's time as real costs, though of other sizes), and several prices: the down product (0.89 us for 0.86 to 0.88, so rival 4 is out); DVE's time a pass (114.9 for 113 to 117); the table loads (33 for about 40); the wait for `resid` (2.67 for 2.9) and the half clock behind it (5.38 for 3.58, where I had added 2); DVE's wait for tanh in slot 20 (2.64 us at 1397.85); E and F within 1 us, with the waits forecast there (in E PE stands 6.24 us for DVE's `bc`, for about 7; in F 4.19 us for GpSimd's join). With `ln_norm` in its old slot D is 15.7 for 16.0 and C 15.5 for 14.7. The rule of the Trainium skill ("TensorE: Matmul & The Clock Gate", Part 3) that stood behind rival 4 is no price here: each product has four weight blocks of its own, and its eight loads of 0.216 us on average stay hidden in the 0.89 us.

**The sum.** 243 us are missing between 2280 and 2523: 12 x (150.86 - 136.9) = 168 in the loop, 56 outside it, 13 since my pass of 133.06 lies 1.06 above the mean, the rest is between execution and median. Of the 168, C and D are 87, A 41, B 28, E and F 12.

1. **The step "C: DVE 9.3, four silu, two gates, and addy1 and stats1".** I listed the moves of `PLAN` and priced those that I saw on DVE. `ln_norm` moved by one slot, on ScalarE behind `in2`, whose Tanh waits for PE, and on GpSimd ahead of the join that FFN 2's last down product needs. GpSimd's queue was not read in the order. DVE's busy time in C was right (14.94 for 14.7); what the step put at nothing is the wait. Price: 79 us (run 1), 7.3 us a pass over my sum for C and D together.
2. **The step "B: from the start of slot 8's input term".** The chain was right: `h1`'s bank comes free 2.46 us behind the start, for 2.4. But PE has then stood for 5.68 us, behind `gate_y` and the silu operation, and slot 9's three products, which the sum has at 3 x 0.86, take 2.3 us more at half clock. I had added 2 us for half clock once, which the convolution behind `resid` uses up (1.8). B is 2.4 us over my sum, and the outproj move takes out 6.4.
3. **The step "A: DVE 26.9 and seven silu operations".** DVE measured 33.3 and not 31.1. 2.4 us are the product with `zs`, moved beside other GpSimd work (3.62 us mean for 1.23; the two operations ahead of it give 0.8 back); and in nearly every second pass A is some 2.4 us longer (34.8 and 37.3 alternate): the scan at its start stands 2.26 us for nothing that the profile shows. The kernel before has such a stand too (second row), but all its passes have 31.6 to 32.2 us in A.

```profile
1292.56 2.29 DVE L887 TENSOR_TENSOR_SCAN hist<-decay,ps_db 128x1024 f32<-128x1024 f32 x1 [2.26 <-issue]
...
1415.38 2.29 DVE L868 TENSOR_TENSOR_SCAN hist<-decay,ps_db 128x1024 f32<-128x1024 f32 x1 [1.97 <-issue]
```

So the change did not bring the stand; it is no longer hidden. Run 9 pays for it too (31.3 and 35.6 us alternate in A), and so does run 14 (29.2 and 33.3). Run 4 warns not to take the product with `zs` as the price: made short again, it gave nothing.
4. **"The partly filled passes I leave alone (±10)".** They cost 56 us. The waits of 1 and 2 and the DVE operations occur in each pass that has a tail or an FFN: in run 3 690 us are outside the loop, in the run without DVE's silu 689.
5. **The forecast's form.** The sum went by stretch and never priced a part of the change by itself, so a part that gains and one that loses could not be told apart. By the runs, each part by itself is (the last two in the new table, the others in the old): loads -125, DVE's silu +190, tokens -46, gates +112, routing sums -16, `ln_norm` +79, `outproj` and `resid` +85: 279 for 289 measured. That they add up this closely is luck, since they overlap: loads and tokens each take D from 20.3 to 14.6, so some 68 us are counted in both, and run 5 gives the silu operations 113 us where run 7 gives 190. Signs and rough sizes are shown, a division of the 289 us is not. Rival 2's claim that silu operations fill DVE's waits "for nothing" is what run 7 denies; the gates' price I had only as two DVE operations of C, not as a bank that is held.

What stays open: how the 80 us between runs 11 and 9 divide further (the gates, `gate_y`, `xT1`, `addy1` were not taken apart in the new table); what the transfer for `x1n` and the output projection on tokens are worth, which no run has alone; and why DVE stands at 1290. The loop's jump back lies there (a turn of the loop is two passes), but no run took it away.

## What to carry to other kernels

Moving work from an engine with waits to one that reads the shared buffers changes who frees these buffers: price the wait of whoever claims them next, and not the operation (here 0.7 us of DVE four times a pass cost 112 us over the run). When a table of slots moves, read the order of every engine that the step has a part on, the quiet ones first; one entry cost 79 us by standing ahead of one join on GpSimd. And undo a change part by part: under its losses this one held a gain of 46 us and one of 16 us that could be had alone.

## What the hardware showed that I had not expected

A 128x1024 product on DVE with all operands in SBUF took 3.99 us beside two GpSimd joins back to back (2.80 us from 1322.13) and 1.23 us one slot earlier (run 4), while the gate products and silu operations, which read PSUM, have means of 0.67 to 0.68 us over all their 704 in the changed kernel. The Trainium skill ("SBUF — State Buffer", section "SBUF: two separate sides") says that an operation of DVE with two operands in SBUF and one of GpSimd that reads SBUF exclude each other for a whole instruction. The trace agrees, except that DVE stood 2.76 us, for both joins and not for one. PE came back from the waits of 5.68 and 5.30 us at half clock and from the one of 2.67 us partly so, which makes a wait cost more than itself: some 2.3 us in the three products behind the first, 1.8 us in the convolution behind the last. And a weight block of its own for each 128 columns cost 0.03 us: eight passes in 0.89 us, for 0.86 with one block for 512 columns.
